# A mixture-of-experts block on one core: the layer-norm gain multiplied into W1 on chip, and its offset added to b1 through TensorE, in place of a stretched token copy for each expert

## The reference, cut to what matters

```python
x = x + conv_attention(_ln_c(x))             # 4 images, 256 tokens of 64 channels
t = _to_tokens(x)
u = _ln_t(t)                                 # what the expert layer reads
logits = u @ Wr + br                         # 8 experts, top 2, softmax weights
xn = (u - mean(u)) * rsqrt(var(u) + 1e-5)    # the same for all experts
xe = xn[None] * ln_g[:, None, :] + ln_b[:, None, :]          # expert e: gain, offset
h = gelu(einsum('end,edh->enh', xe, W1) + b1[:, None, :])    # 64 -> 256
y = einsum('enh,ehd->end', h, W2) + b2[:, None, :]           # 256 -> 64
t = t + sum of the two chosen y, weighted
```

## Time and profile before

| what | value |
|---|---|
| median of 3 runs | 59.06 us (58.34 to 59.18) |
| the profiled execution | 58.3 us, of which 56.5 us span |
| TensorE matmul busy | 50.0 us, 88% |
| VectorE busy | 41.6 us, 74% |
| ScalarE busy | 35.2 us, 62% |
| GpSimd busy | 24.8 us, 44% |
| granted TensorE clock | 0.99 of full |

### The profile page before, as it was taken

The page is one execution under the profiler, slowest core; times in us unless marked ns, Lnnn a source line. Parts: engine busy times, 40 slices in busy tenths (PEclk is TensorE's granted clock), DMA queues, the critical chain, the costliest instruction groups (busy, mean ns, idle before and its releaser), DMA issues.

```text
span 56.5 us, 1641 instructions
## 1 busy us (share of the span) xinstructions
PE 50.0 (88%) x556; PEld 29.9 (53%) x556; DVE 41.6 (74%) x175; ACT 35.2 (62%) x79; POOL 24.8 (44%) x49
## 2 busy tenths in 40 slices
PE   0995999998789999999999969999999999959920
PEld 0332756895666986762483724754746633306610
DVE  3199689697999798998289999197480799399630
ACT  4500468990794959979879697497897890610000
POOL 6239680000069899939189920006859000710000
PEclk9999999999999999999999999999999999999995
DMA  0441456974000000000000371366897103000012
GB/s 0 99 117 24 100 131 184 381 259 157 0 17 0 0 0 0 0 12 6 0 11 7 142 199 53 123 191 225 273 280 193 28 6 93 0 0 0 0 40 52
DMA packets 4585, 4.80 MB, mean 85 GB/s; under 512 B 2205, under 2 KB 3041, under 8 KB 4577
## 3 DMA queue, kind: packets, MB, share of 16 engines
q1 hardware_dynamic: 4256, 4.67, 27.2%
q10 hardware_dynamic: 320, 0.03, 0.7%
HBM read 4.41 MB, written 0.29 MB: 83 GB/s over the span
## 4 chain that ended last, share of the span: by engine, by line
PE 63%; DVE 21%; issue 5%; DMA 3%; POOL 1%; ACT 1%; DVEq 0%; POOLq 0%
PE banks L1057 18%; PE banks L1085 13%; PE banks L991 4%; PE banks L1038 4%; PE banks L964 4%; PE banks L1127 3%; DMA X<-in_x_dram 3%; PE banks L1098 3%; PE banks L943 2%; DVE PTS L613 2%; DVE HG L757 2%; PE banks L1141 2%; PE banks L927 2%; PE banks L951 1%; DVE nmax L608 1%
## 5 line engine op out<-in xcount | busy, mean ns | idle before, releaser
L492 ACT ACTIVATE H<-banks,PF 128x512 f32<-128x512 f32 x32 | 19.6, 687 | 4.0 <-PE banks L1057 3.3
L1057 PE MATMUL banks<-XE,W1F 64*64 64x256 f32 x224 | 14.1, 380 | 0.0
L1057 PEld LDWEIGHTS banks<-XE,W1F 64*64 64x64 f32 x224 | 9.2, 133 | 4.7 <-issue 3.1
L385 POOL TENSOR_TENSOR acc<-acc,gated 128x512 f32<-128x512 f32 x4 | 5.5, 1368 | 11.4 <-DVE gated L747 6.5
L1085 PE MATMUL banks<-H,W2F 64*64 64x512 f32 x80 | 9.7, 596 | 0.4 <-issue 0.4
L368 POOL TENSOR_SCALAR XE<-XF,PF,LB 128x256 f32<-128x256 f32 x14 | 7.7, 562 | 1.4 <-ACT XF L470 1.4
L736 DVE TENSOR_TENSOR YS<-banks,YA 128x512 f32<-128x512 f32 x5 | 3.4, 690 | 4.7 <-ACT YA L502 4.7
L346 POOL TENSOR_TENSOR rs<-base,half 128x2 f32<-128x2 f32 x4 | 2.8, 700 | 8.6 <-DVE base L649 8.3
L927 PE MATMUL banks<-zeros 128*128 128x512 f16 x13 | 4.9, 507 | 1.3 <-POOL zeros L387 1.3
L1085 PEld LDWEIGHTS banks<-H,W2F 64*64 64x64 f32 x80 | 3.1, 132 | 4.0 <-issue 3.9
L453 ACT ACTIVATE PR<-banks,nmax 128x256 f32<-128x256 f32 x8 | 3.8, 480 | 1.7 <-DVE nmax L608 1.7
(11 more groups left out here) (93 smaller groups left out, 81.2 us busy)
## 6 DMA issues: line engine op xcount, KB each, us to landing
GS<-gates_kept SPq DMA_DIRECT2D x14, 128.0 KB, 3.3
W1F<-in_w_dram SPq DMA_DIRECT2D x1, 768.0 KB, 4.4
W2F<-in_w_dram SPq DMA_DIRECT2D x1, 512.0 KB, 4.8
G<-gates_kept SPq DMA_DIRECT2D x2, 256.0 KB, 4.1
W1F<-in_w_dram SPq DMA_DIRECT2D x1, 256.0 KB, 3.4
out_dram<-res SPq DMA_DIRECT2D x4, 64.0 KB, 1.7
X<-in_x_dram SPq DMA_DIRECT2D x2, 64.0 KB, 1.9
X<-in_x_dram SPq DMA_DIRECT2D x1, 128.0 KB, 2.4
```

The lines of the kernel that those rows point to most:

```text
L385: nc.gpsimd.tensor_tensor(acc[h][:, :], acc[h][:, :], gated[s % 2][:, :], ALU.add).then_inc(acc_ready, 1)
L492: nc.scalar.activation(H[:, r, :].rearrange("p (t n) -> p t n", t=PT), ps_z[z_slot(g // J)][:, :, PIX * j:PIX * j + PIX], ACT.Gelu, bias=P ...
L1057: mm = nc.tensor.matmul(ps_z[z_slot(q)][C * c:C * c + C, k, PIX * j:PIX * j + PIX], W1F[rows, e, j, C * c:C * c + C], XE[h][rows, e, :], s ...
```

## The change

XE and all stretches are gone. GpSimd instead multiplies W1 of each expert by its ln_g once (scale_weights: W1G, 128x256 each, eight of them), six before second_pow(0) and two after router_pow(0); add_bias(1) is moved ahead of them. TensorE multiplies W1 by ln_b (shift_bias: 32 matmuls of 64 rows, 64 columns and one moving column), VectorE adds b1 (two additions: B1G), and gelu takes its offset from there. Layer 1 of every expert reads XF. In TensorE's list shift_bias stands behind turn_b2, and turn_x2(0) has moved ahead of turn_probs(3). values(3) is now ScalarE's and stands between exps(2) and exps(3); values(2) has moved ahead of exps(2).

```diff
+            def scale_weights(e):
                 pool.wait_ge(ffn_in, 16)
-                pool.wait_ge(lb_in, 32)
-                pool.wait_ge(XF_ready, IMG * (h + 1))
-                nc.gpsimd.tensor_scalar(XE[h][:, e, :], XF[h][:, :, :].rearrange("p i n -> p (i n)"),
-                                        PF[:, F_G + e:F_G + e + 1], LB[:, e:e + 1],
-                                        ALU.mult, ALU.add).then_inc(xe_ready, 1)
+                pool.wait_ge(w1_in[0 if e < 2 else 1], 16)
+                nc.gpsimd.tensor_scalar(W1G[:, e, :, :], W1F[:, e, :, :], PF[:, F_G + e:F_G + e + 1], None, ALU.mult)\
+                    .then_inc(w1g_ready, 1)
...
+            def shift_bias():
+
+                pe.wait_ge(w1_in[0], 16)
+                pe.wait_ge(w1_in[1], 16)
+                pe.wait_ge(lb_in, 32)
+                pe.wait_ge(V_kept[2], 1)
+                pe.wait_ge(V_kept[3], 1)
+                for e in range(E):
+                    for c in range(2):
+                        for j in range(J):
+                            rows = slice(C * j, C * j + C)
+                            mm = nc.tensor.matmul(ps_b1[j][C * c:C * c + C, e:e + 1], W1F[rows, e, j, C * c:C * c + C],
+                                                  LB[rows, e:e + 1], start=True, stop=True)
+                            if e == E - 1:
+                                mm.then_inc(b1_ps, 1)
...
+            def shift_bias():
+
+                dve.wait_ge(ffn_in, 16)
+                for j in range(J):
+                    dve.wait_ge(b1_ps, 2 * J)
+                    nc.vector.tensor_tensor(B1G[:, :, j], ps_b1[j],
+                                            PF[:, F_B1:F_B1 + UNITS].rearrange("p (e j) -> p e j", j=J)[:, :, j],
+                                            ALU.add).then_inc(b1_ready, 1)
...
             def layer1_first(q, i):
-                pe.wait_ge(w1_in[0], 16)
+                pe.wait_ge(w1g_ready, q + 1)
+                pe.wait_ge(XF_ready, i + 1)
...
-                                  W1F[rows, q, j, C * c:C * c + C], XE[0][rows, q, P * i:P * i + P],
+                                  W1G[rows, q, j, C * c:C * c + C], XF[0][rows, i, :],
```

More of the change, by code:

```diff
@@ L100, in build_block @@
         ps_y = [banks[:, 4 + k, :] for k in range(2)]
+        ps_b1 = [banks[:, j, 0:E] for j in range(J)]
         ps_b2 = banks[:, 3, 0:PAIRS]
@@ L117, in build_block @@
         W1F = sb("W1F", [P, E, J, P])
+        W1G = sb("W1G", [P, E, J, P])
+        B1G = sb("B1G", [P, E, J])
         W2F = sb("W2F", [P, UNITS, C])
@@ L150, in build_block @@
         XF = both("XF", [P, IMG, P])
-        XE = both("XE", [P, E, PIX])
         inv2 = both("inv2", [P, TILES])
@@ L232, in build_block @@
         XF_ready = sem("XF_ready")
-        xe_first = sem("xe_first")
-        xe_ready = sem("xe_ready")
+        w1g_ready = sem("w1g_ready")
+        b1_ps = sem("b1_ps")
+        b1_ready = sem("b1_ready")
         L_ps = sem("L_ps")
@@ L362, in add_bias @@
                                         ALU.add).then_inc(xv_ready, 1)
-            def stretch(h, e):
+            def scale_weights(e):
                 pool.wait_ge(ffn_in, 16)
-                pool.wait_ge(lb_in, 32)
-                pool.wait_ge(XF_ready, IMG * (h + 1))
-                nc.gpsimd.tensor_scalar(XE[h][:, e, :], XF[h][:, :, :].rearrange("p i n -> p (i n)"),
-                                        PF[:, F_G + e:F_G + e + 1], LB[:, e:e + 1],
-                                        ALU.mult, ALU.add).then_inc(xe_ready, 1)
-            def stretch_second(i):
-                pool.wait_ge(ffn_in, 16)
-                pool.wait_ge(lb_in, 32)
-                pool.wait_ge(XF_ready, i + 1)
-                nc.gpsimd.tensor_scalar(XE[0][:, 1, P * i:P * i + P], XF[0][:, i, :],
-                                        PF[:, F_G + 1:F_G + 2], LB[:, 1:2], ALU.mult, ALU.add).then_inc(xe_second, 1)
+                pool.wait_ge(w1_in[0 if e < 2 else 1], 16)
+                nc.gpsimd.tensor_scalar(W1G[:, e, :, :], W1F[:, e, :, :], PF[:, F_G + e:F_G + e + 1], None, ALU.mult)\
+                    .then_inc(w1g_ready, 1)
             def add_up(s):
@@ L402, in _ @@
             first_pow(3)
+            add_bias(1)
+            for e in range(6):
+                scale_weights(e)
             second_pow(0)
@@ L405, in _ @@
             router_pow(0)
-            stretch_second(0)
-            add_bias(1)
-            stretch_second(1)
-            stretch(0, 2)
-            stretch(0, 3)
+            scale_weights(6)
+            scale_weights(7)
             second_pow(2)
-            for e in range(4, E):
-                stretch(0, e)
             second_pow(3)
             router_pow(1)
-            for e in range(E):
-                stretch(1, e)
             add_up(1)
@@ L485, in gelu @@
                 u, r, j = g % UNITS, g % RING, g % J
+                act.wait_ge(b1_ready, J)
                 if g < 2 * J:
@@ L525, in _ @@
             probs(1, 1)
+            values(2)
             exps(2)
-            values(2)
+            values(3)
             exps(3)
             probs(2, 0)
-            stretch_first(0)
             turn_x2(0)
@@ L863, in _ @@
             probs(2, 1)
+            shift_bias()
             second_norm(1)
@@ L867, in _ @@
             probs(3, 0)
-            values(3)
-            stretch_first(1)
             turn_x2(1)
@@ L1045, in layer1 @@
                 h, e = q // E, q % E
-                pe.wait_ge(w1_in[0 if e < 2 else 1], 16)
-                pe.wait_ge(xe_ready, q - 1)
+                pe.wait_ge(w1g_ready, e + 1)
+                pe.wait_ge(XF_ready, IMG * (h + 1))
                 if q == 2:
@@ L1057, in layer1 @@
                             mm = nc.tensor.matmul(ps_z[z_slot(q)][C * c:C * c + C, k, PIX * j:PIX * j + PIX],
-                                                  W1F[rows, e, j, C * c:C * c + C], XE[h][rows, e, :],
+                                                  W1G[rows, e, j, C * c:C * c + C],
+                                                  XF[h][rows, :, :].rearrange("p i n -> p (i n)"),
                                                   start=True, stop=True)
@@ L1171, in _ @@
             turn_b2()
+            shift_bias()
+            turn_x2(0)
             turn_probs(3)
-            turn_x2(0)
             attend(2)
```

19 lines of the change are left out of this document (2 added, 17 removed).

## The result

The changed kernel takes 59.81 us (59.25 to 60.36, 4 runs), the kernel before, beside it, 58.7 (58.24 to 59.18, 4 runs). The ratio is 1.020 [1.014, 1.025]: some 1.1 us slower, where 0.25 less was forecast, and just above the range's upper end of 59.8. That it is slower is clear of the noise; whether by more than 2% is not.

A forecast was written before the change was run, and what follows sets the result against it. TensorE was taken to bound the kernel (63% of the chain, VectorE 21%). The terms -0.6 + 0.2 + 0.15 = -0.25, carried to the median of 59.06, gave 58.8 us, range 58.0 to 59.8.

The forecast's parts named there:

- The gain at 33 us: At layer2_split(2): route(1) without GpSimd's stretches beside it frees 1.25 us on VectorE, of which 0.6 reaches the end.
- Rival A: route(1) isn't freed, its long instructions having another cause; +0.2 us, 59.25; chance 0.17.
- The offset's length: TensorE's 32 offset matmuls, 64 instructions in the trace's count, behind turn_b2: 0.9 us from about 16.35.
- Its way to layer2_split(2): The offset starts attend(2) and the first gelu 0.28 us later; 0.2 late goes on to layer2_split(2).
- Rival B: Offset matmuls take 1.6 to 1.7 us and hold up the turn from attention to experts; 59.5 to 60.2; chance 0.14.
- Its upper bound of 1.7: Length of the 64 offset instructions at the pace of layer1_first, 0.026 us each.
- The multiplication's price: GpSimd's multiplications of W1 ahead of second_pow(0): 0.56 us each, the last four ending at 14.2, at no cost.
- The 1.8 of slack: Time on GpSimd between the multiplications' end at 14.2 and second_pow(0) at 15.96, as cover.
- Rival C: The second power waits for W1, landing after 13.7 in place of 11.9; at 15.2, 60.3; chance 0.04.
- The early contention: GpSimd's multiplications slow VectorE at 9 to 14 us, by image 3's pair: 0.15 us, range 0 to 0.8.
- The step that failed: The loop behind layer2_split(2) keeps its turn of 3.64 us, the change touching none of its links; no cost.
- 58.05 and 56.25: Forecast for the profiled execution and its span, from 58.3 and 56.5 before.

The follow-up runs named there:

- e1: Kernel before, with GpSimd holding back the second half's last six stretches until route(1)'s gates are ready; 57.98 us, 0.989 of the kernel before.
- a1: The changed kernel run again, unaltered; 60.06 us, 1.025 of the kernel before.
- d1: The changed kernel with GpSimd's eight multiplications written in different forms, some with an added zero; ran once, 59.4 us.
- a2: The changed kernel without the offset matmuls, VectorE copying b1 as it is; 58.9 us, 1.005 of the kernel before.
- c4: The changed kernel with 16 offset matmuls of 64 rows by 128 columns in place of 32 of 64 by 64; 60.99 us, 1.041.
- c2: Kernel before, with 32 one-column matmuls ahead of the first transposition and two warming matmuls fewer; 61.46 us, 1.047.
- c3: The changed kernel with an added 0.0 in the multiplications and expert 1 of the first half in one piece; 59.15 us, 1.007.
- c1: The changed kernel with 32 more one-column matmuls ahead of the first transposition and two warming matmuls fewer; 62.35 us, 1.040.
- e2: c3 with warming matmuls in 32 bits and three small matmuls ahead of each of the two last layer2_split; 58.84 us, 1.000.
- e4: e2 with 32 moving columns in place of one in each offset matmul; 58.17 us, 0.994 of the kernel before.
- e3: c4 with 64 moving columns, all the same, in place of one; 59.65 us, 1.018 of the kernel before.
- b1: Kernel before, with add_bias(1) moved ahead and six early GpSimd multiplications of W1 that nobody reads; 58.61 us, 1.004.

## Why the prediction was wrong, point by point

**The gain at 33 us: right.** Forecast 1.25 freed on VectorE and 0.6 at the end. e1 does only this and has 0.62 in the second stretch and 0.67 in all (1.1% of 58.57). Rival A, that route(1) isn't freed, is ruled out by it. The prediction left open how the stretches lengthen those steps. The rows show it: each long step ends just behind a stretch. The long members of the four kinds end 0.55 apart, at 31.19, 31.74, 32.30 and 32.85; the eight stretches take 0.55 each, and the last ends at 28.45 + 4.36 = 32.81. The Trainium skill, page SBUF — State Buffer, section Who interferes with whom, says of the SBUF ports that VectorE and GpSimd share that whoever issues first holds them for its whole instruction, and the other is blocked. These rows agree, and so does HG, which ended 0.56 behind GpSimd's addition in before and in a1.

**The offset's length: right. Its way to layer2_split(2): right in size, wrong in cause.** 0.9 forecast, 1.04 to the next start. The second stretch should have become shorter by 0.6 - 0.2 = 0.4, and is by 0.50 in a1 and 0.51 in d1. ScalarE's first gelu starts 0.18 later behind turn_b2 than before (4.59 against 4.41), where 0.28 was forecast. But it does so in a2 as well (4.58), which has no offset: attend(2) comes 0.19 later there too. Both kernels have turn_probs(3) behind turn_x2(0), which has to wait for second_norm either way (its pair ends at 17.95 in a1, and turn_x2(0) starts at 18.01). So the 0.2 that the sum gave to the offset goes with the new order; no run tried the old order with the offset, or changed the order alone. Rival B needed 1.3 for the offset. Its upper bound of 1.7 divides 1.17 by 45 steps, where 48 loads have 47; 1.6 would be right, and nothing hangs on it. The rule of 60 cycles for a matmul (the Trainium skill, page TensorEngine Tiling (Array Packing), section Instruction Overhead) would have given 1.6 here, and the trace speaks against it. What a1 and c4 show is a price of 0.0145 for an instruction on four tiles and of 0.053 on two.

**The multiplication's price: wrong, without harm.** The step read 0.56 from the stretch; the form with one operation takes 0.93. The 1.8 of slack were used up to within 0.1. Rival C didn't come.

**The early contention: right in size.** 0.15 forecast; image 3's pair took 0.34 longer and turn_b2 started 0.13 to 0.19 later (changed, d1). Of a1's 0.68, 0.61 are there when VectorE copies the first keys, and so are all of a2's 1.0: that is the slower warm-up above, not contention. No profile of the kernel before shows a warm-up as slow as a1's, but e1's, with the same attention code, is 0.3 late, and 70 executions of the kernel before spread from 56.4 to 57.5 in their spans at full clock.

**The step that failed** is the one that put nothing behind layer2_split(2), neither in the span nor around it: "The loop afterwards keeps its 3.64: its links are layer 2, keep_part and sum_parts, none of which the change touches." The loop does keep it (34.06 to 37.73 in a1, 3.67). But the sum carried this on to the end of the span, and there the change does touch something that no list of its instructions names: 64 more matmuls in the trace's count bring a fifth fetch of 16 KB, and it comes while the output is being written. That costs 0.3 in the changed kernel's profile, 0.95 in a1's and d1's, 0.7 in c2 and 0.4 in c3, by where it falls; and nothing in c1, e2 and e4, where it came earlier, or in a2, c4 and e3, where it didn't come. These sizes are from one profile of each kernel. The second half of the same step was to carry the 1.8 around the span over unchanged ("58.05 and 56.25"); it measured 2.16, so 0.36 of the 1.1 lost is there.

For a1 against before the account of the span is: +0.68 ahead of turn_b2, -0.50 to layer2_split(2), +0.44 to the last addition (HG), +0.95 for the output, in all 1.57 of the 1.6 between the spans. Of this the 0.61 of the warm-up isn't the change's, as far as the rows show. d1 has neither the slow warm-up nor the wait at HG, and is the cleaner account: +0.13, -0.51, +0.03 and +0.95, in all 0.60, and 0.5 outside the span. Without the last two terms it would have been faster than the kernel before by 0.35, near the 0.25 forecast.

**What it left out as well** is the clock. The profile before has it at 0.99, and the prediction took it for given. In the kernel before it didn't fall in any of 70 executions (0.989 at the least). In the changed kernel it fell in one of four, behind 64 matmuls of one column; the second stretch is 18.84 there against a1's 17.24, 1.6 longer. This is not in the ratio, but in the times that a user sees.

**Open** stays what the 0.36 outside the span is: the extra packet on q14 comes with it in all fourteen kernels, and no run takes the two apart. Open too is the wait for the gates, which moved GpSimd's addition onto HG in a1 and e3 (0.4) and not in the others. It wasn't tried by itself. What makes the clock fall isn't settled either: a2, which has no offset matmuls, showed it in two of ten executions, b1 in one of ten, a1 in none of four. And no run tried the powers on another engine than GpSimd.

## What to carry to other kernels

Before adding many small instructions to an engine, look at the instruction queue's row on the page and at when its last packet moves: one packet more beside the last output can cost more than the instructions. Compare the time with the span as well: here a third of the loss lay outside the span. Take the price of an operation from a row with the same operands and number of operations, not only the same shape. And before a rewrite that frees an engine from contention, try to move the contending work by one wait: here that gave 0.6 us, and no form of the rewrite gave more.

## What the runs showed of the hardware that was not expected

- A packet of instructions on q8 is 16 KB and holds one DMA engine for 0.9 to 1.4 us; the last packets of an output beside it lasted up to 58 to 156 ns in place of 20 to 27. With 556 and 588 matmuls (and as many loads) there were four fetches, with 604 to 682 five.
- GpSimd's tensor_scalar of 128x256 in 32 bits takes 0.92 with one operation and 0.48 with a second one that adds a constant 0.
- Matmuls with one moving column come ahead of a fall of the granted clock to 1.2 GHz: on four tiles (0.9 us of them) in 1 of 8 executions of the changed kernel and a1, 2 of 12 of c3, 6 of 13 of e2 and 3 of 4 of c1, on two tiles (1.7 us) in 5 of 5 of c4. c2, with such matmuls only ahead of the first transposition, shows none in four. Without any it is none of 70 of the kernel before and of e1's six, but also 2 of 10 of a2 and 1 of 10 of b1, so they aren't its only cause. With 64 columns at c4's pace it is 0 of 4 (e3), with 32 on four tiles 0 of 12 (e4), for 0.03 us more.
